# Two attentions and two FFNs on one core: slot 1 of the second attention loaded in the last chunk, FFN transposes between output products, all units of that attention with their values in one visit

## What is computed

```python
x = x + _L0_attn_a_ref(_layernorm(x), Wq, Wc, Wk, Wv, Wo)         # 32 heads of 16, rotary, full softmax
x = x + _L0_ffn_ref(_layernorm(x), lora_A, lora_B, W, bias, lora_weights)
x = x + _L0_attn_b_ref(_layernorm(x), w_attn, b_attn, w_proj, b_proj)
x = x + _L0_ffn_ref(_layernorm(x), lora_A, lora_B, W, bias, lora_weights)
```

## Time and profile before

| | us |
|---|---|
| median of 3 runs (1803.03 to 1814.71) | 1810.11 |
| the profiled execution | 1811.41 |
| its span on the core | 1809.6 |
| PE, DVE, ACT, POOL busy in the span | 1662.6, 1390.8, 973.4, 142.8 |
| mean granted PE clock | 0.955 of full |

### The profile page before, as it was taken

One profiled execution on the slowest core, in us unless ns is written; L12 is line 12 of the kernel. 1 busy time (PEld: TensorE's weight loads), 2 busy tenths in 40 slices (PEclk: granted clock), 3 DMA queues, 4 the chain that ended last, 5 costly groups with the idle time before them and its releaser, 6 DMA issues. The chain is left out here.

```text
span 1809.6 us, 32945 instructions
## 1 busy us (share of the span) xinstructions
PE 1662.6 (92%) x13040; PEld 857.5 (47%) x13040; DVE 1390.8 (77%) x3007; ACT 973.4 (54%) x1103; POOL 142.8 (8%) x224
## 2 busy tenths in 40 slices
PE   6898999999999999999889998959999999999697
PEld 4554333333333333333246677624545454554486
DVE  3776799999999999999176444727898989885585
ACT  3432377777777777777421111124666666667210
POOL 3332200000000000000000000030000000003000
PEclk9999699999999999999989999957999999999799
DMA  6776334333333333330532246463464554542221
GB/s 215 222 176 198 65 65 89 62 60 65 55 55 55 55 58 54 55 54 11 167 109 71 69 140 189 128 113 56 89 100 74 92 83 82 89 76 68 98 75 70
DMA packets 116857, 167.58 MB, mean 93 GB/s; under 512 B 20828, under 2 KB 58092, under 8 KB 116588
## 3 DMA queue, kind: packets, MB, share of 16 engines
q1 hardware_dynamic: 114880, 160.17, 39.0%
q0 software_dynamic: 1824, 5.31, 1.4%
HBM read 100.41 MB, written 64.50 MB: 91 GB/s over the span
## 5 line engine op out<-in xcount | busy, mean ns | idle before, releaser
L354 DVE TENSOR_REDUCE mxp<-ps_m 128x1 f32<-128x512 f32 x1280 | 799.5, 686 | 70.6 <-PE ps_m L320 64.9
L671 ACT ACTIVATE a_p<-a_ps_s 128x1024 f32<-128x1024 f32 x512 | 522.9, 1026 | 148.8 <-PE a_ps_s L591 136.6
L671 ACT ACTIVATE b_p<-b_ps_s 128x1024 f32<-128x1024 f32 (+1 forms) x320 | 295.0, 939 | 188.2 <-PE b_ps_s L591 184.8
L351 DVE CUSTOM_DVE_ANT_0 ps_m<-ps_m,b_masks 128x128 f32<-128x128 f32 (+3 forms) x512 | 240.3, 518 | 77.1 <-PE ps_m L320 74.4
L320 PE MATMUL ps_m<-slot_qk 62*128 62x512 f32 (+3 forms) x624 | 239.2, 468 | 28.6 <-DMA slot_qk<-alibi_rows 17.0
L320 PE MATMUL ps_m<-a_slot_qk 62*128 62x512 f32 x640 | 238.2, 450 | 0.8
L591 PE MATMUL a_ps_s<-a_slot_qk 64*128 64x512 f32 x640 | 232.3, 443 | 1.2
L615 PE MATMUL a_ps_o<-a_p,a_slot_v 128*32 128x256 f32 x2560 | 205.6, 390 | 9.9 <-ACT a_p L671 5.4
L591 PEld LDWEIGHTS a_ps_s<-a_slot_qk 64*128 64x128 f32 x640 | 96.2, 185 | 128.9 <-issue 123.1
L591 PE MATMUL a_ps_s<-slot_qk 64*128 64x512 f32 x384 | 136.2, 454 | 0.6
L320 PEld LDWEIGHTS ps_m<-slot_qk 62*128 62x128 f32 x624 | 106.2, 200 | 59.3 <-DVE mxp L354 27.0
(11 more groups left out here) (209 smaller groups left out, 2294.5 us busy)
## 6 DMA issues: line engine op xcount, KB each, us to landing
va_groups<-w_o SPq DMA_DIRECT2D x16, 512.0 KB, 3.7
ka_parts<-pa_parts SPq DMA_DIRECT2D x16, 512.0 KB, 3.9
qa_parts<-pa_parts SPq DMA_DIRECT2D x32, 256.0 KB, 3.7
kb_parts<-slot_memory SPq DMA_DIRECT2D x16, 512.0 KB, 3.5
qb_parts<-slot_memory SPq DMA_DIRECT2D x32, 256.0 KB, 3.9
vb_groups<-w_proj SPq DMA_DIRECT2D x16, 512.0 KB, 3.2
a_slot_qk<-qa_parts SPq DMA_DIRECT2D x60, 128.0 KB, 4.2
a_slot_qk<-ka_parts SPq DMA_DIRECT2D x48, 128.0 KB, 6.9
```

The lines of the kernel that those rows point to most:

```text
L351: dve.tensor_tensor_reduce(from_, from_, mask_of_query[:, CHUNK - keys:], 1.0, LOWEST, ALU.add, ALU.max, accum_out=to).then_inc(piece_take ...
L354: dve.tensor_reduce(to, from_, AX.X, ALU.max).then_inc(piece_taken, 1)
L671: act.activation(p_sb[:, (2 * u + pair) % NP, :, off:CHUNK], ps_s[:, 2 * pair:2 * pair + 2, off:CHUNK], ACT.Exp, scale=scale).then_inc(exp ...
```

## The change

Slot 1 of the second attention gets memory of its own: its queries and keys use words that the FFN's `xn` and `xnt` of the middle stage (and `xn` and the low part of Wq in `project_a`) use before, its values those of the first attention's output sums. POOL clears it after the last FFN product of chunk 3, and SP loads its shares in the last chunk, after each of the eight stores. In the attention only slot 2 is left to begin (now on `slot_memory`), by POOL and SP at its start. `SKIP` is gone: the first step spreads its pieces over all ten units as the others do. `values` makes all units of the causal attention in part 1, in one visit; the first attention keeps two. In both uses of `output_and_ffn` the FFN's transposes of chunk k - 1 stand between the second and the third output product of chunk k, on PE and in the list that sets the banks. The first product after transposes waits for each quarter just before it uses it (also in `project_a`). The last stage's split buffers use the slots' memory.

```diff
-    def load_share(self, e, i, q_d, k_d, v_d, alibi_d, ones_d):
+    def load_share(self, e, i, g, q_d, k_d, v_d, alibi_d, ones_d):
...
             r, tile = divmod(i, PAIR)
-            self.load_q_row(e, r, tile, q_d, 0, self.all_loaded)
-            self.load_k_row(e, r, tile, k_d, 0, self.all_loaded)
+            self.load_q_row(e, r, tile, q_d, g, self.all_loaded)
...
         elif i == rows:
-            self.load_v(e, v_d, 0, self.all_loaded)
+            self.load_v(e, v_d, g, self.all_loaded)
...
             if self.al:
-                self.load_alibi(e, alibi_d, 0, self.all_loaded)
+                self.load_alibi(e, alibi_d, g, self.all_loaded)
...
     AT_ONCE = early.pieces == NPC
-    SKIP = 3 if AT_ONCE else 0
-    before_unit_of_first = [0] * SKIP + [2 * round(NPC * sum(columns[SKIP:u]) / sum(columns[SKIP:]) / 2)
-                                         for u in range(SKIP, NU + 1)]
...
     def loads(g):
-        return g // SLOTS + (1 if g % SLOTS else 0)
+        return g // SLOTS + (1 if g % SLOTS >= READY else 0)
...
-                if j:
-                    pe.wait_ge(rows_set[j - 1], SETS)
-                    pe.wait_ge(first_loaded[j - 1], K_LOAD)
-                wait_past(pe, qk_loaded[j], loads(g) * LOAD - (K_LOAD if j else 0))
+                if j >= READY:
+                    pe.wait_ge(rows_set[j], SETS)
+                    pe.wait_ge(first_loaded[j], K_LOAD)
+                elif g:
+                    slots[j].wait_loaded(pe)
+                wait_past(pe, qk_loaded[j], loads(g) * LOAD - (K_LOAD if j >= READY else 0))
...
-                for g in range(1, SLOTS):
-                    slots[g].clear(pool, cleared)
-                pool.wait_ge(cleared, 1)
-                slots[1].load_k(pool, k_d, 1, alibi_d, first_loaded[0])
+                for g in range(READY, SLOTS):
+                    slots[g].clear(pool, cleared[g])
+                pool.wait_ge(cleared[READY], 1)
+                slots[READY].load_k(pool, k_d, READY, alibi_d, first_loaded[READY])
...
-                pool.wait_ge(cleared, 2)
-                pool.wait_ge(shift_loaded, 2 * SHIFT)
-                pool.wait_ge(first_loaded[0], K_LOAD)
-                slots[2].load_k(pool, k_d, 2, alibi_d, first_loaded[1])
+                for g in range(READY + 1, SLOTS):
+                    pool.wait_ge(cleared[g], 1)
+                    pool.wait_ge(shift_loaded, 2 * SHIFT)
+                    pool.wait_ge(first_loaded[g - 1], K_LOAD)
+                    slots[g].load_k(pool, k_d, g, alibi_d, first_loaded[g])
...
                 early.stores.wait(sp, B)
                 def begin(g):
-                    sp.wait_ge(cleared, g)
-                    slots[g].set_rows(sp, ones_d, rows_set[g - 1])
+                    sp.wait_ge(cleared[g], 1)
+                    slots[g].set_rows(sp, ones_d, rows_set[g])
...
-                begin(1)
+                begin(READY)
...
                     qh, blocks = units[u]
                     (kt, off, n, at) = blocks[0]
-                    if n == CHUNK:
+                    if not causal:
                         ranges = [(kt, off + part * CHUNK // 2, CHUNK // 2, at + part * CHUNK // 2)]
...
                                            p_sb[:, (2 * u + h // 2) % NP, h % 2, at:at + n],
-                                           start=(u == first_of[qh] and part == 0), stop=last)
+                                           start=(u == first_of[qh] and part == int(causal)), stop=last)
...
                 def step(s, j):
                     for u in range(NU):
-                        before = before_unit if s else before_unit_of_first
-                        lo, hi = AHEAD + before[u], AHEAD + before[u + 1]
+                        lo, hi = AHEAD + before_unit[u], AHEAD + before_unit[u + 1]
...
-def split_products(pe, out, lhs, rhs, pieces, between=None):
+def split_products(pe, out, lhs, rhs, pieces, between=None, before_piece=None):
...
+        if before_piece and (a, b) == (0, 0):
+            before_piece(kc)
         mm = pe.matmul(out, lhs[a](kc), rhs[b](kc), start=(n == 0), stop=(n == len(steps) - 1))
...
-                for task in turn_tasks[c]:
-                    banks.wait_drained(pe, task)
                 task = ("latent", c)
                 banks.wait_empty(pe, task)
                 split_products(pe, banks.out(task)[0:LATENT, :], [lambda kc: wc_high[:, kc, :], lambda kc: wc_low[:, kc, :]],
-                               x_parts, KC).then_inc(banks.fill(task), 1)
+                               x_parts, KC, None, lambda kc: banks.wait_drained(pe, turn_tasks[c][kc])
+                               ).then_inc(banks.fill(task), 1)
...
     order = []
     for k in range(STEPS):
+        if k < NC:
+            order += [("o", k, t) for t in range(TPC // 2)]
         if 0 <= k - 1 < NC:
             order += f_turns[k - 1]
         if k < NC:
-            order += [("o", k, t) for t in range(TPC)]
+            order += [("o", k, t) for t in range(TPC // 2, TPC)]
...
+            o_parts = [env["first_qk"][:, half].rearrange("p (k t) -> p k t", k=KC) for half in halves]
             o_high_ready = sem("o_high_ready")
             o_split = sem("o_split")
-            f_xnt = [sb(f"f_xnt{n}", [P, KC, CHUNK], F32R) for n in range(2)]
+            f_xnt = [env["second_qk"][:, half].rearrange("p (k t) -> p k t", k=KC) for half in halves]
...
-                            first.load_share(sp, i, env["qb_d"], env["kb_d"], env["vb_d"],
+                            first.load_share(sp, i, 0, env["qb_d"], env["kb_d"], env["vb_d"],
                                              env["alibi"], env["ones"])
+                        if c == NC - 1:
+                            if i == 0:
+                                sp.wait_ge(second.cleared, 1)
+                            second.load_share(sp, i, 1, env["qb_d"], env["kb_d"], env["vb_d"],
+                                              env["alibi"], env["ones"])
                     if c == NC - 1:
...
-            def natural(kind, c, lhs, weights, cols=slice(0, D)):
...
+                for t in tiles:
                     task = (kind, c, t)
                     banks.wait_empty(pe, task)
                     tokens = slice(t * P, (t + 1) * P)
+                    def turned(kc):
+                        if turns and t == tiles[0]:
+                            banks.wait_drained(pe, turns[kc])
                     if len(weights) > 1:
                         mm = split_products(pe, banks.out(task), [lambda kc, x=x: x[:, kc, tokens] for x in lhs],
                                             [lambda kc, x=x: x[:, kc, cols] for x in weights], KC,
-                                            between(c, PT + t) if kind == "v" else None)
+                                            between(c, PT + t) if kind == "v" else None, turned)
                     else:
                         for kc in range(KC):
+                            turned(kc)
                             mm = pe.matmul(banks.out(task), lhs[0][:, kc, tokens], weights[0][:, kc, cols],
                                            start=(kc == 0), stop=(kc == KC - 1))
                     mm.then_inc(banks.fill(task), 1)
...
             for k in range(STEPS):
+                def products(tiles):
+                    natural("o", k, o_parts if fast else [output.o_sb[:, k % 2]], w_out, tiles=tiles)
+                if k < NC:
+                    pe.wait_ge(o_split if fast else output.o_scaled, KC * (k + 1))
+                    products(range(TPC // 2))
                 if 0 <= k - 1 < NC:
                     f_norm.transposes(pe, banks, k - 1, f_turns[k - 1], ident)
                 if k < NC:
-                    pe.wait_ge(o_split if fast else output.o_scaled, KC * (k + 1))
-                    natural("o", k, o_parts if fast else [output.o_sb[:, k % 2]], w_out)
+                    products(range(TPC // 2, TPC))
                 if nxt and 0 <= k - 2 < NC:
                     q_norm.transposes(pe, banks, k - 2, q_turns[k - 2], ident)
                 c = k - 1
                 if 0 <= c < NC:
-                    for task in f_turns[c]:
-                        banks.wait_drained(pe, task)
-                    natural("f", c, f_xnt, w_eff)
+                    natural("f", c, f_xnt, w_eff, turns=f_turns[c])
                 c = k - 2
                 if nxt and 0 <= c < NC:
...
-                    for task in q_turns[c]:
-                        banks.wait_drained(pe, task)
...
+                        def turned(kc):
+                            if m == 0:
+                                banks.wait_drained(pe, q_turns[c][kc])
                         at = (m + KC) % PT * P
                         split_products(pe, banks.out(task), [lambda kc, x=x: x[:, kc, at:at + P] for x in w_qkv],
                                        [lambda kc, x=x: x[:, kc, :] for x in q_xnt], KC,
```

(24 more changed lines are left out.)

57 lines of the change are left out of this document (30 added, 27 removed).

## The result

The changed kernel takes 1790.25 us in the median (1787.80 to 1795.52, 4 runs), the kernel before 1811.12 beside it: a ratio of 0.9895, 95% interval 0.9855 to 0.9935. The prediction was 1788. Repeated in another series it took 1794.98 beside 1812.56, ratio 0.9907 (0.9877 to 0.9937). So it is faster by about 1%, as forecast; but several terms behind the sum were wrong, and it was luck that their errors nearly cancelled.

A forecast was written before the change was run, and what follows sets the result against it. PE bounded the kernel, losing 17 us to a gap and 21 to the clock in group 0 of the second attention. Terms -26.0 + 5.6 + 2.3 - 1 - 3 + 0 = -22.1 gave 1788 us, range 1772 to 1805.

The forecast's parts named there:

- 2 (clock low through group 0): Second attention: clock stays low through group 0 and visits cost 0.6 a group; sum -10.8, about 1799 us; chance 0.21.
- 3 (the visits win): Attention groups: one-visit values win what PE alone says, -13.5 in place of +5.6; 1770 us; chance 0.06.
- 5 (the gap stays): Start of second attention: slot 1 isn't ready at its use and PE's gap remains; about 1812 us; chance 0.04.
- Rival 1: Group 0, second attention: clock returns early or hardly falls; term -34 to -38, 1776 to 1780 us; chance 0.18.
- Rival 4: Second attention: longer visits starve DVE, 2.5 us a group, +38 over 15 groups; sum +18.8, 1829 us; chance 0.05.
- Slot 1 early: Group 0, second attention: loading slot 1 in chunk 3 removes the 17.0 us gap; -26.0, bounds -17.5 and -38.3.
- h: Group 0, second attention: time from its start until the clock rises, taken as 29.6 us from the first attention.
- Values in one visit: Second attention: one 512-column visit instead of two makes DVE run dry; +0.4 x 14 = +5.6, bounds -13.5 and +11.
- Transposes in the middle stage: Middle stage, chunk 0: f(0,0) still waits for DVE's residual add and the clock falls; +2.3, bounds 0 and +5.
- Waits by quarter, chunk 3: Middle stage, chunk 3: earlier start, first product done at 1128.1 and not 1131.4; -3, bounds -5 and 0.
- Last stage: Last stage: transposes +1.7, chunks 2 and 3 wait about 1 us each, quarters gain; sum 0, bounds -3 and +4.
- The projections: Projections: PE starts after DVE's first low part, but every engine has slack; -1, bounds -2.1 and 0.

The follow-up runs named there:

- the best kernel: Changed kernel with values in two visits, the old order of transposes and GpSimd's clear of slot 1 ahead of the norm: 1773.77 us, ratio 0.9815.

## Why the prediction was right, and where it was not

**The sum** said -22.1, the medians say -20.9. Right in sign, size and range, but the size was luck. In the two profiles of the changed kernel slot 1 gave 8.5 and 7.1 us more than its term, and the values took 6.4 and 7.3 more than theirs; the middle stage took 4.7 and 3.9 more than the +2.3 - 3, and the last stage 3.1 and 0. The spans' differences are -15.9 and -19.4, the second series' medians give -17.6. Of the rivals, 2 (clock low through group 0), 3 (the visits win) and 5 (the gap stays) are out; 1 and, in part, 4 happened together.

**Slot 1 early** was forecast at -26.0 with bounds -17.5 and -38.3; it is -33.1 to -34.5. The 17.0 us went whole, as said. The step that failed is h, how long the clock stays low after the first scores: the prediction took 29.6 us from the first attention's start, and it is 9 to 17 us in eleven profiles (in the first of the changed kernel 9.1 us, from 1182.25 to 1191.4). With h = 9.1 and 12.7 the prediction's own formula gives 33.1 and 34.6 us for the group, where 33.1 and 34.5 were measured; so the model held and its input did not. The first attention was not as near in kind as it looked. PE is busy there from 184 us, but for 20 us with maxima and plain products of 256 columns alone; its first scores come at 203.66 (203.91 in the kernel before), and the clock is back at 211.7, 8 us after them:

```profile
202.51 1.22 PE L650 MATMUL a_ps_s<-x_sb 128*128 128x256 f32 x2
203.66 0.79 PE L594 MATMUL a_ps_s<-slot_qk 64*128 64x512 f32 x1
```
```profile
199.00:211.70 12.70, 12.66 (x50) 5.47 (x54) 9.18 (x15) 3.99 (x4) 0.00 (x0) 0.50 0.53 104
211.70:215.00 3.30, 3.30 (x36) 1.26 (x32) 3.10 (x6) 2.81 (x3) 0.00 (x0) 0.99 0.00 0
```

In thirteen of the fourteen profiles it is 5.7 to 8.1 us, in one 2.0. Counted from the first scores, as in the second attention, the same row would have given h of 8 us, a group of 32.6 us and a term of -35. No run changed what PE does ahead of the first scores there, so why the clock stays low through that work is not shown. Rival 1 described what happened, with a price of -34 to -38. The other row for a long stretch, the 20 us at 1220 to 1240 in the earlier trace rows, belongs to a kernel that had stood still for 17 us; the run with the sparse first units gives 20 us from the first scores. Why it was 40 us of busy time in the one profile of the kernel before is not settled. The Trainium skill (TensorE: Matmul & The Clock Gate, Part 1) says that activity releases the throttle; the estimate of near -34 that the prediction set beside this rule is what was measured (-33.1 and -34.5).

**Values in one visit** was forecast at +5.6 with bounds up to +11; it is +12.0 and +12.9; the second holds 0.9 us of the new wait in the third step, the first only 0.1. The mechanism was right and is now shown: during a visit of 1.00 us VectorE runs out of maxima, and with VectorE lighter the cost is gone. The term was mis-sized: +0.4 a step from walking one group through with mean durations, where the runs say +0.9. The walk set three reductions of 0.62 us against a visit, those of pieces 512 wide; at the visit shown above two of the three pieces left are 128 wide and last half as long. That this accounts for the whole difference is not shown. The forecast's mark for "wrong", a step over 30.5 us, was not reached; its "right", 29.5 to 29.9, was missed. Rival 4, which had this mechanism at 2.5 us a step, had a good third of its size.

**Transposes in the middle stage.** Right in cause and size: f(0,0) at 927.43 for a forecast of about 928.1, held by VectorE's residual add, and 5.93 - 3.60 = 2.3 us for the clock. With the order undone the eight matmuls take 3.60 us again.

**Waits by quarter, chunk 3.** Forecast -3; the stretch from chunk 3's start to the attention's stays as it was (52.8 us for 52.6), and the start is later. The step that failed took VectorE's low parts as fixed at 1123.35; they begin at 1128.43. The quarter waits do their part: PE starts 1.04 us after them and not 2.78. But ahead stands a chain that the prediction didn't look at: the clear stretches the norm by 3.2 us, stores begin later, SP issues chunk 2's values after all shares of slot 0, at 1121.21 and not 1114.10, and VectorE waits 10.10 us for the first of them. Of these 7.1 us, 1.5 lay ahead of the norm (it starts at 1095.41 and not 1093.90) and 3.2 are the stretch. The other 2.4 are not explained: in the first profile of the best kernel, with the clear out of the way and the norm at 1093.81, SP still issues the values only at 1116.91. "The memory is free some 30 us before the first load" was true, and what the clear would lie over was not asked.

**Last stage.** Forecast 0 (-3 to +4); measured +3.1 and 0.0, with the order at +4.3 and the rest, the quarter waits above all, at about -3 (130.3 before, 127.5 in the mean with the old order and quarter waits). The waits of "about 1 us each" are 1.04 and 1.11, the last wait 2.26 for 4.17. So the items were sized about right: the order's came to 3.7 (1.7 and twice 1) and measure 4.3, the last wait's to 2 or 4.5. The two profiles of the changed kernel have the same waits there and differ by the clock, 0.88 and 0.92 of full in the stage (0.89 before).

**The projections** -1: -0.5 and -2.4 with the whole first attention in it, not told apart; the same code comes to this point between 880.3 and 885.9 us in the profiles, so this term was not measured.

## What to carry to other kernels

Where an engine reads from a few buffers that another fills, ask for the longest piece of other work between two fills, and not only for the sum: a merge that saves its producer 0.15 us in each of six units made the step 0.9 us longer here. Count what the buffers hold at that very place; narrow pieces last the reader less. A sum that comes out right can hide terms worth undoing; price each part by a stretch of the profile that holds it alone, and undo the parts one at a time. When work moves to another stage, ask for each instruction of it, also a clear on an idle engine, what it will lie beside.

## What was not expected of the hardware

- A GpSimd clear of 128 x 4096 words (3.5 us) holds up VectorE's normalizing step (one input and the output in SBUF, 128x512, four times): 5.08 us in place of 1.92. It is the first instruction that stands, 3.72 us in place of 0.55; it begins just after the clear, and the three behind it are as short as ever:

```profile
1095.41 3.72 DVE L850 TENSOR_SCALAR mid_q_xn<-x_sb,mid_q_mv,mid_q_rstd 128x512 f32<-128x512 f32 x1 [1.13 <-POOL mid_q_rstd L855]
```

VectorE's addition with two inputs in SBUF keeps its 2.49 us for four beside the clear (the run with the clear first). The Trainium skill (SBUF — State Buffer, section "SBUF: two separate sides") has both: GpSimd shares a port pair with VectorE instructions in a two-port mode, whoever comes second is blocked for the whole instruction, and an instruction with two inputs is blocked only by a GpSimd one that reads. The traces agree, though they do not show the mode of the instruction.
- Products with 32 output rows at four places of the array run side by side: two heads of 512 columns take 0.98 us, four take 1.00. The Trainium skill (TensorEngine Tiling (Array Packing), section Tiling Modes) lists this shape with four tiles and says that tiles operate independently; the trace agrees.
- The granted clock rises 9 to 17 us after the first scores of the second attention in the eleven profiles with slot 1 early, maxima in all units and no extra products, with PE busy 95% of group 0 (31.44 of 33.09 us), and not always at the same point for the same code (9.1 us in one profile of the changed kernel, 12.7 in the other). In its first attention the same kernel has it back 8.1 us after the first scores, but stays at half clock for the 20 us of maxima and 256-column products ahead of them, with PE busy 14.29 of 15 us from 184 to 199.
